# Attention scores in three bf16 parts on 64 rows a head, where it was two fp32 parts on 32 rows

## The chip, the cores and the metric

One core of one Trainium2 chip runs the whole program. The metric is the time of one execution in microseconds of device time, median of the runs. Lower is better.

## The reference

Two transformer layers on x of 4 x 512 x 128 with 16 heads of width 8. Layer 0 has causal attention and a top-1 expert network, layer 1 has self-attention, a "recursive" attention of its output to two stored past states, a gate, and a top-2 expert network. Only the two attentions matter here. Cut to that:

```python
# layer 0, for each of 4 batches and 16 heads, T = 512, dh = 8
q, k, v = split(h @ Wqkv.T)
dots = einsum('bhid,bhjd->bhij', q, k) * dh ** -0.5
attn = softmax(where(causal_mask, -inf, dots))
x = x + ga * (einsum('bhij,bhjd->bhid', attn, v) @ Wout.T + bout)
# layer 1
scores = einsum('bhsd,bhtd->bhst', q, k) * SCALE          # not causal
output = (softmax(scores) @ v) @ Wo + bo
rq = output @ Wrq + brq                                     # from the output of self-attention
rscores = einsum('bhsd,pbhtd->pbhst', rq, past @ Wrk + brk) * SCALE   # two past states of 256
rctx = mean over p of softmax(rscores) @ (past @ Wrv + brv)
```

## The kernel before

The program is one hand-written order of phases (`plan()`), which every engine walks through in turn and issues its own part of; the engines wait for each other by semaphores. `play` steps through generators: a `yield` ends a step, and a generator's start step is a number of STEPS0, STEPS1, FRONT, BACK, KPREP and QPREP (lines 18 to 73). So a phase is due at a step, not at a time.

Attention goes by units: four heads of one batch. Layer 0 has 16 units, layer 1 has 32, of which 16 are recursive (L1_SEQ: self 0, self 1, rec 0, self 2, rec 1, self 3, rec 2, rec 3, four units each). A unit takes 16 steps. It has two halves, which run on different units at the same time:

- `front`: 16 plain scores, phase `mx` (tile t of 128 queries, head j), into a PSUM bank of the ring of four; VectorE reduces each to row maxima (line 2206, recursive line 2199; in layer 0 line 2203, a custom operation that adds the mask, with a read of its accumulator). Then `mcol` splits the maxima in a high and a low part on VectorE, `mT` transposes them on TensorE, ScalarE evicts them to Ms, and `mput` on SP writes them by DMA into rows of the query tile Qs (line 1224).
- `back`: 16 transposed scores, phase `st` (chunk c of 128 keys, head j), which wait for the maxima in Qs, into three PSUM banks; ScalarE takes the exponential to Et (line 1623); in layer 0 GpSimd cuts the diagonal (line 1386); then the value matmuls `pv` and `pva` (line 1898), four heads side by side in columns of 32.

In layer 0 front starts at step 16u + 10 and back at 16u + 35; in layer 1 at 12 and 40.

A head's 8 numbers are made into 32 rows, so that one fp32r matmul sums all the products of high and low parts: rows 0 to 7 high, 8 to 15 low and 16 to 23 high in the queries (for the keys high, high, low), and rows 24 up hold the maxima in the queries and -1 in the keys. The parts are made thus: ScalarE evicts the projection to Xq or Xk, VectorE masks the low 12 bits away (`high`, line 2060, phase `split`), GpSimd subtracts (phase `low`, lines 1327 and 1330, in two halves), SP writes three pieces to Dq or Dk in DRAM (`stage`, lines 1174 to 1183), and reads a unit's four heads back as 128 rows (`ldq`, `ldk`).

In layer 1 keys lie in KT (or RKT for past states) as 4 x 32 rows and head j's matmul uses rows 32j to 32j + 31 alone. In layer 0 they lie block-diagonally in Kbd, three tiles of 128 x 4 x 512 that GpSimd clears at the start; a head's `st` takes all 128 rows of Kbd and Qs, zeros included, and so does its `mx`. Four DMAs a unit fill one Kbd tile.

The first unit of each layer takes no way over DRAM: extra projections `k0`, `q0` (`k1`, `q1`) with weight columns laid out as the 32 rows (u0, u1) go through ScalarE (U0k, U0q) and VectorE (T, lines 2152 to 2175) into Kbd 0 or KT 0 and Qs 0. ScalarE copies three heads and GpSimd one to Kbd (`k0put`). The past keys are split by VectorE (`pastkv`) into kst, doubled by GpSimd (`past2`) and transposed to RKT in four phases `pastK`.

The lines of the score matmuls:

```python
r = slice(32 * j, 32 * j + 32) if l else slice(0, 128)
keys = RKT[r, g, :] if kind == "rec" else KT[u % NK][r, :] if l else Kbd[u % 3][:, j, :]
nc.tensor.matmul(bank(ph)[:, q0:512], keys[:, c * 128:(c + 1) * 128], Qs[q_no(l, u) % NQ][r, q0:512], ...)
```

## Time and profile before

| | us |
|---|---|
| median of 3 runs | 945.59 |
| lowest, highest | 942.89, 954.91 |
| profiled execution | 943.85 |
| its span, first to last instruction | 942.1 |
| attention of layer 0 | 38 to 250 |
| experts of layer 0 | 250 to 332 |
| attention of layer 1, with the start of it | 332 to 795 |
| experts of layer 1 | 795 to 942 |

In the profile PE is TensorE's matmuls, PEld its weight loads, DVE is VectorE, ACT ScalarE, POOL GpSimd and SP the queue of SyncE; a q behind an engine's name is its instruction queue, such as one that issues DMAs. Times are us from the span's start unless marked ns. "idle before" is the time in which the engine stood still just ahead of an instruction, and behind the arrow is what ended that. The ends of matmuls are modelled, so the spacing of starts says more than the durations. PEclk is the share of 2.4 GHz that TensorE's clock was granted; there are two levels, 1 and 0.5. Each unit of either layer takes some 13 us.

### The profile page before, as it was taken

The numbers are of one execution on the slowest core, as the hardware profiler recorded it, in microseconds if no ns is written. First come the engines' busy times: TensorE is split into PE (matmuls) and PEld (weight loads), VectorE is DVE, ScalarE is ACT, GpSimd is POOL, SyncE is SP. The second block draws the span as 40 slices with busy tenths as digits, with TensorE's granted clock in tenths as the row PEclk, the third lists the DMA queues.
The fourth block names the chain that finished last, engine by engine and source line by source line (L and its number), as shares of the span: only waits on it lengthen the run. The fifth ranks groups of instructions, "written<-read, shape, count | busy, mean of one in ns | idle before, by whom it ended". The sixth has DMA issues, their size and how long they took to land.

```text
span 942.1 us, 18341 instructions
## 1 busy us (share of the span) xinstructions
PE 834.8 (89%) x6319; PEld 501.3 (53%) x6319; DVE 720.9 (77%) x2077; ACT 546.7 (58%) x1202; POOL 282.3 (30%) x424
## 2 busy tenths in 40 slices
PE   7698999888879869999999999999987989898994
PEld 6354655455579733344344434344432434788994
DVE  5777788887265768898899888989895874786674
ACT  2355656546556524688788868687664765333431
POOL 6233334326412354204210011001025223344332
PEclk9799999998979966799999979799795988988997
DMA  5556523111103133244242403110251100102123
GB/s 156 189 169 195 179 80 108 41 47 36 43 21 96 56 102 125 72 160 145 112 151 69 136 25 105 47 58 25 83 177 51 47 7 21 42 27 78 42 64 113
DMA packets 68470, 82.43 MB, mean 87 GB/s; under 512 B 8295, under 2 KB 44391, under 8 KB 68057
## 3 DMA queue, kind: packets, MB, share of 16 engines
q1 hardware_dynamic: 40120, 46.11, 16.2%
q10 hardware_dynamic: 24960, 28.32, 9.6%
q0 software_dynamic: 3296, 6.82, 2.2%
...
q14 instruction: 44, 0.35, 0.1%
...
## 4 chain that ended last, share of the span: by engine, by line
PE 55%; DVE 27%; issue 4%; DMA 4%; ACT 4%; POOL 3%; another core or an unknown queue 1%; SPq 1%; ACTq 1%; DVEq 0%; POOLq 0%
PE pv L1898 13%; PE st L1875 10%; DVE M L2199 9%; PE ring L2013 6%; PE ring L1866 5%; PE ring L1769 4%; DVE M L2206 4%; PE st L1998 4%; DVE ring L2203 3%; ACT Et L1623 2%; PE ring L1837 2%; PE st L2006 2%; PE st L1991 2%; PE pv L2006 2%; PE ring L1780 1%
## 5 line engine op out<-in xcount | busy, mean ns | idle before, releaser
L1623 ACT ACTIVATE Et<-st 128x512 f32<-128x512 f32 (+3 forms) x768 | 372.9, 545 | 149.8 <-PE st L1875 130.1
L2206 DVE TENSOR_REDUCE M<-ring 128x1 f32<-128x512 f32 x256 | 159.4, 683 | 29.8 <-PE ring L1866 23.6
L2199 DVE TENSOR_REDUCE M<-ring 128x2 f32<-128x512 f32 x256 | 159.9, 681 | 15.4 <-PE ring L1866 14.7
L1898 PE MATMUL pv<-Et,Va 128*32 128x256 f32 (+3 forms) x1536 | 146.5, 443 | 4.0 <-ACT PVs L1630 2.3
L2203 DVE CUSTOM_DVE_ANT_0 ring<-ring,maskw 128x128 f32<-128x128 f32 (+3 forms) x256 | 120.5, 512 | 36.0 <-PE ring L1866 33.5
L1875 PE MATMUL st<-Qs,Kbd 128*128 128x512 f32 (+3 forms) x256 | 90.0, 370 | 8.9 <-ACT Et L1623 7.5
L1898 PE MATMUL pv<-Et,RV 128*32 128x256 f32 x1024 | 92.4, 434 | 5.1 <-ACT PVs L1630 5.0
L1866 PE MATMUL ring<-Kbd,Qs 128*128 128x128 f32 (+3 forms) x256 | 84.6, 360 | 13.5 <-DVE M L2203 5.9
L1386 POOL TENSOR_SCALAR_AFFINE_SELECT Et<-Et 128x256 f32<-128x256 f32 x128 | 53.0, 419 | 128.0 <-ACT Et L1623 127.7
L1866 PE MATMUL ring<-RKT,Qs 32*128 32x512 f32 x256 | 84.4, 540 | 3.9 <-DVE M L2199 2.3
L1866 PE MATMUL ring<-KT,Qs 32*128 32x512 f32 x256 | 79.0, 553 | 8.9 <-DVE M L2206 8.3
L1875 PE MATMUL st<-Qs,RKT 32*128 32x512 f32 x256 | 78.2, 549 | 5.7 <-ACT Et L1623 5.7
L1875 PE MATMUL st<-Qs,KT 32*128 32x512 f32 x256 | 79.6, 547 | 0.1
L2013 PE MATMUL ring<-w2d,hbuf 128*128 128x128 f32 x552 | 75.4, 282 | 0.7 <-issue 0.7
L1875 PEld LDWEIGHTS st<-Qs,Kbd 128*128 128x128 f32 x256 | 49.2, 195 | 49.9 <-ACT Et L1623 33.1
L2013 PEld LDWEIGHTS ring<-w2d,hbuf 128*128 128x128 f32 x552 | 70.2, 199 | 1.2 <-issue 1.2
L1898 PEld LDWEIGHTS pv<-Et,Va 128*32 128x32 f32 x1536 | 33.8, 112 | 60.9 <-issue 43.5
L1866 PEld LDWEIGHTS ring<-Kbd,Qs 128*128 128x128 f32 x256 | 49.9, 200 | 28.1 <-DVE M L2203 14.3
L1461 POOL DMA_INDIRECT Zd<-Yt,dst x39 | 41.8, 1072 | 65.4 <-ACT Yt L1745 63.7
L1424 POOL DMA_INDIRECT Xd<-fh,pos x48 | 47.6, 991 | 36.2 <-DVE pos L2521 17.4
L1875 PEld LDWEIGHTS st<-Qs,RKT 32*128 32x128 f32 x256 | 32.2, 200 | 46.5 <-issue 25.4
L1327 POOL TENSOR_TENSOR Xq<-Xq,hq 128x256 f32<-128x256 f32 x24 | 18.9, 803 | 123.7 <-DVE hq L2060 121.8
...
## 6 DMA issues: line engine op xcount, KB each, us to landing
...
```

Of the source, the lines that this page charges most:

```text
L1386: e.affine_select(diag, diag, [[0, 2], [1, 128]], ALU.is_ge, 0.0, base=0, channel_multiplier=-1).then_inc(cut_done, 1)
L1424: e.indirect_dma_start(Xd1 if l else Xd0[g], bass.IndirectOffsetOnAxis(r["pos"][:, i, n:n + 1], 0), B.fh[PARTS[q][n // 4]][:, n % 4, :], N ...
L1461: e.indirect_dma_start(Zd, bass.IndirectOffsetOnAxis(B.dst[:, k:k + 1], 0), B.Yt[n % 4][:, :], None).then_inc(y_stored[1][n % 4], 16)
L1623: e.activation(Et[s // 2 % 4][:, j % 2, q0:512], bank(ph)[:, q0:512], ACT.Exp, scale=SCALE).then_inc(exp_done, 1)
L1769: ins = nc.tensor.transpose(bank(ph)[:, t * 128:(t + 1) * 128], src(t), ident[:, :])
L1866: nc.tensor.matmul(bank(ph)[:, 0:n], Qs[q_no(l, u) % NQ][r, t * 128:(t + 1) * 128], keys[:, 0:n], start=True, stop=True).then_inc(mx_full, 1)
L1875: nc.tensor.matmul(bank(ph)[:, q0:512], keys[:, c * 128:(c + 1) * 128], Qs[q_no(l, u) % NQ][r, q0:512], start=True, stop=True).then_inc(st ...
L1898: ins = nc.tensor.matmul(pv[32 * j:32 * j + 32, cols], v, Et[s // 2 % 4][:, j % 2, cols], start=first and (l == 0 or what == "pva"), stop= ...
L2013: ins = nc.tensor.matmul(bank(ph)[:, 0:128], B.hbuf[n % 3][:, f, :], B.w2d[weight_set(l, n)][:, f, :], start=(f == 0), stop=(f == 3))
L2199: e.tensor_reduce(M[i][:, t, j, :], bank(ph)[:, :].rearrange("p (two n) -> p two n", two=2), AX.X, ALU.max).then_inc(mx_red, 1)
L2203: e.tensor_tensor_reduce(bank(ph)[:, 0:n], bank(ph)[:, 0:n], maskw[:, 512 - n:512], 1.0, -3e38, ALU.add, ALU.max, M[i][:, t, j, 0:1]).then ...
L2206: e.tensor_reduce(M[i][:, t, j, 0:1], bank(ph)[:, 0:n], AX.X, ALU.max).then_inc(mx_red, 1)
```

## The change

A number is now the sum of three bf16 parts. A head has 64 rows: for each of its 8 numbers eight rows, six of them for the products of parts that are kept (QPARTS, KPARTS), one (MAXROW) for the maxima, which have three parts too, one empty. Two heads lie in the 128 rows of a tile and two more behind them in the free dimension (Qs, KT and RKT are 128 x 2 x 512 in bf16, as many bytes as before). Layer 0 uses the same KT tiles as layer 1; Kbd with its clearing, its four loads a unit and `k0put` is gone. The order of `mx` and `st` and the steps of front and back stay as they are.

VectorE's `split` makes the first part by a copy to bf16, GpSimd's `low` subtracts, a new phase `mid` on VectorE copies the second part, a new phase `last` on GpSimd subtracts for the third. For the first batch of each layer VectorE does all eight operations within `split`. Each part is written once for all its places by a DMA that repeats it (3, 2 and 1 times). The first unit of each layer is made from the parts on chip by `sel`: three matmuls with a 0/1 matrix (`pick`) for each half of queries and keys; ScalarE evicts the keys and adds the -1 row (kcol), VectorE the queries. `mT` is now a matmul on the upper halves of the fp32 words, and `mput` has three DMAs, six for recursive units, where it had two and four.

```diff
+QPARTS, KPARTS = (0, 0, 0, 1, 1, 2), (1, 0, 2, 0, 1, 0)
+HR, MAXROW = 64, 6
...
-        for piece in range(6 if keys else 3):
-            if piece < (4 if keys else 2):
-                do("low", l, b, k, piece)
-            do("stage", l, b, k, piece)
+        if k == 0:
+            for piece in (0, 3, 1, 4, 2, 5):
+                do("stage", l, b, k, piece)
+                yield
+            return
+        for side in range(1 + keys):
+            do("low", l, b, k, 2 * side)
+            do("low", l, b, k, 2 * side + 1)
+            do("stage", l, b, k, 3 * side)
             yield
+        if keys:
+            yield
+        do("mid", l, b, k)
+        yield
+        for side in range(1 + keys):
+            do("last", l, b, k, 2 * side)
+            do("last", l, b, k, 2 * side + 1)
+            do("stage", l, b, k, 3 * side + 1)
+            yield
+        for side in range(1 + keys):
+            do("stage", l, b, k, 3 * side + 2)
...
-    do("clear", "Kbd0")
-    do("clear", "Kbd1")
     do("hT", 0, 0)
     do("warm", 2)
     do("brow", 1)
-    do("k0")
-    do("q0")
-    for what in ("pq", "pk"):
+    for what in ("pq", "pk", "split"):
         do(what, 0, 0, 0)
-    do("k0put")
+    for s in range(2):
+        do("sel", 0, "k", s)
+        do("sel", 0, "q", s)
...
-            do("pastK", g)
-            yield from wait((6, 14, 4, 4)[g])
+            for s in range(2):
+                do("pastK", g, s)
+                yield from wait((3, 7, 2, 2)[g])
...
+        def rows_of(j):
+
+            return slice(HR * (j % 2), HR * (j % 2) + HR)
...
-                    if piece in (0, 1):
+                    of = (Dq[k % 2] if piece < 3 else Dk[n % 2]).rearrange("h (r a) n -> (h r) a n", a=8)
+                    if piece == 0:
                         sp.wait_ge(q_high, n + 1)
-                        e.dma_start(Dq[k % 2][:, 16 * piece:16 * piece + 8, :], hq[:, :]).then_inc(q_staged, 16)
+                        e.dma_start(of[:, 0:3, :], Pq[0][:, :].unsqueeze(1).broadcast_to([128, 3, 512])).then_inc(q_staged, 16)
+                    elif piece == 1:
+                        sp.wait_ge(q_mid, n + 1)
+                        e.dma_start(of[:, 3:5, :], Pq[1][:, :].unsqueeze(1).broadcast_to([128, 2, 512])).then_inc(q_staged, 16)
                     elif piece == 2:
-                        sp.wait_ge(q_low, 2 * n + 2)
-                        e.dma_start(Dq[k % 2][:, 8:16, :], Xq[:, :]).then_inc(q_staged, 16)
-                    elif piece in (3, 4):
+                        sp.wait_ge(q_last, 2 * n + 2)
+                        e.dma_start(of[:, 5, :], Pq[2][:, :]).then_inc(q_staged, 16)
...
-                    wide = 4 if units[l][u][0] == "rec" else 2
+                    many = 2 if units[l][u][0] == "rec" else 1
                     q = Qs[q_no(l, u) % NQ]
                     sp.wait_ge(*taken(("mT", l, u)))
-                    for m in range(wide):
-                        e.dma_start(q[24 + m:128:32, :].bitcast(F32), Ms[l][u % 2][16 * m:16 * m + 16, :]).then_inc(m_in[u % 2], 16)
+                    for m in range(NPART * many):
+                        m16 = 32 // many * m
+                        e.dma_start(q[8 * m + MAXROW:128:HR, :, :], Ms[l][u % 2][m16:m16 + 16, :]).then_inc(m_in[u % 2], 16)
...
+                elif what == "last":
+                    l, b, k, piece = a
+                    n0 = 256 * (piece % 2)
+                    sl = slice(n0, n0 + 256)
+                    if piece < 2:
+                        pool.wait_ge(q_mid, n_split["split", l, b, k] + 1)
+                        e.tensor_tensor(Pq[2][:, sl], Xq[:, sl], Pq[1][:, sl], ALU.subtract).then_inc(q_last, 1)
+                    else:
+                        pool.wait_ge(k_mid, n_ksplit["split", l, b, k] + 1)
+                        e.tensor_tensor(Pk[2][:, sl], Xk[:, sl], Pk[1][:, sl], ALU.subtract).then_inc(k_last, 1)
...
+                elif what == "sel":
+                    l, of, s = a
+                    pe.wait_ge(ld["pick"], 16)
+                    if of == "k":
+                        pe.wait_ge(k_last, 2 * n_ksplit["split", l, 0, 0] + 2)
+                    else:
+                        pe.wait_ge(q_last, 2 * n_split["split", l, 0, 0] + 2)
+                    parts, n0 = (Pq, 0) if of == "q" else (Pk, 6)
+                    for i in range(NPART):
+                        ins = nc.tensor.matmul(bank(ph)[:, :], pick[:, n0 + 3 * s + i, :], parts[i][0:32, :], start=(i == 0),
+                                               stop=(i == NPART - 1))
+                    ins.then_inc(misc_full, 1)
...
-                    nc.tensor.transpose(bank(ph)[:, 0:128], Mc[l][u % 2][:, :], ident[:, :]).then_inc(misc_full, 1)
+                    parts = M[:, u % 2:u % 2 + NPART, :].rearrange("p i n -> p (i n)")
+                    nc.tensor.matmul(bank(ph)[0:96, 0:128], tops(parts), tops(ident[:, :]), start=True, stop=True).then_inc(misc_full, 1)
...
-                    keys = RKT[r, g, :] if kind == "rec" else KT[u % NK][r, :] if l else Kbd[u % 3][:, j, :]
+                    r, s = rows_of(j), j // 2
+                    keys = RKT[r, g, s, :] if kind == "rec" else KT[u % NK][r, s, :]
                     pe.wait_ge(*m_ready(l, u))
-                    nc.tensor.matmul(bank(ph)[:, q0:512], keys[:, c * 128:(c + 1) * 128], Qs[q_no(l, u) % NQ][r, q0:512],
+                    nc.tensor.matmul(bank(ph)[:, q0:512], keys[:, c * 128:(c + 1) * 128], Qs[q_no(l, u) % NQ][r, s, q0:512],
...
-                    high(hq[:, :], Xq[:, :]).then_inc(q_high, 1)
-                    if has_keys(l, k):
-                        n = n_ksplit[ph]
+                    e.tensor_copy(Pq[0][:, :], Xq[:, :]).then_inc(q_high, 1)
+                    if nk is not None:
                         dve.wait_ge(*taken(("pk", l, b, k)))
-                        if n:
-                            dve.wait_ge(k_staged, 48 * n)
-                        high(hk[:, :], Xk[:, :]).then_inc(k_high, 1)
+                        if nk:
+                            dve.wait_ge(k_staged, 48 * nk)
+                        e.tensor_copy(Pk[0][:, :], Xk[:, :]).then_inc(k_high, 1)
+                    if k == 0:
+                        dve.wait_ge(q_high, n + 1)
+                        e.tensor_tensor(Xq[:, :], Xq[:, :], Pq[0][:, :], ALU.subtract).then_inc(q_low, 2)
+                        dve.wait_ge(k_high, nk + 1)
+                        e.tensor_tensor(Xk[:, :], Xk[:, :], Pk[0][:, :], ALU.subtract).then_inc(k_low, 2)
+                        dve.wait_ge(q_low, 2 * n + 2)
+                        e.tensor_copy(Pq[1][:, :], Xq[:, :]).then_inc(q_mid, 1)
+                        dve.wait_ge(k_low, 2 * nk + 2)
+                        e.tensor_copy(Pk[1][:, :], Xk[:, :]).then_inc(k_mid, 1)
+                        dve.wait_ge(k_mid, nk + 1)
+                        e.tensor_tensor(Pk[2][:, :], Xk[:, :], Pk[1][:, :], ALU.subtract).then_inc(k_last, 2)
+                        dve.wait_ge(q_mid, n + 1)
+                        e.tensor_tensor(Pq[2][:, :], Xq[:, :], Pq[1][:, :], ALU.subtract).then_inc(q_last, 2)
...
+                elif what == "mid":
+                    l, b, k = a
+                    sp_ = ("split", l, b, k)
+                    dve.wait_ge(q_low, 2 * n_split[sp_] + 2)
+                    e.tensor_copy(Pq[1][:, :], Xq[:, :]).then_inc(q_mid, 1)
+                    if sp_ in n_ksplit:
+                        dve.wait_ge(k_low, 2 * n_ksplit[sp_] + 2)
+                        e.tensor_copy(Pk[1][:, :], Xk[:, :]).then_inc(k_mid, 1)
...
-                    halves(hi, lo, M[u % 2][:, :, :, :] if kind == "rec" else M[u % 2][:, :, :, 0]).then_inc(mcol_done, 1)
+                    step(e.tensor_tensor(m1, m0, tops(m0), ALU.subtract))
+                    settle()
+                    e.tensor_tensor(m2, m1, tops(m1), ALU.subtract).then_inc(mcol_done, 1)
...
-                    halves(k4[:, t, :, 8:16], k4[:, t, :, 16:24], bank(ph)[:, 0:128].rearrange("p (h r) -> p h r", r=8))
+                    settle()
+                    step(e.tensor_copy(k4[:, :, 1], keys))
+                    settle()
+                    step(e.tensor_tensor(pastR[:, :], keys, k4[:, :, 1], ALU.subtract))
+                    settle()
+                    step(e.tensor_copy(k4[:, :, 0], pastR[:, :]))
+                    settle()
+                    step(e.tensor_tensor(k4[:, :, 2], pastR[:, :], k4[:, :, 0], ALU.subtract))
```

## Rows read from the trace of the kernel before

**Rows 1.** The page: the span, busy time by engine, and TensorE's clock in 40 slices

```profile
span 942.1 us, 18341 instructions
...
PE 834.8 (89%) x6319; PEld 501.3 (53%) x6319; DVE 720.9 (77%) x2077; ACT 546.7 (58%) x1202; POOL 282.3 (30%) x424
...
PEclk9799999998979966799999979799795988988997
```

**Rows 2.** Busy time by stage: stretch, length, us (instructions) by engine, PEclk, DMA share, GB/s

```profile
38.00:250.00 212.00, 187.81 (x1202) 112.72 (x1201) 160.08 (x672) 122.27 (x332) 84.18 (x168) 0.96 0.34 100
...
360.00:795.00 435.00, 409.26 (x3414) 175.35 (x3414) 370.77 (x813) 314.80 (x608) 84.72 (x118) 0.88 0.26 85
```

**Rows 3.** Chain that ended last, by line: first 38 to 250, then 360 to 795

```profile
by line: PE st L1875 12.1%; PE pv L1898 11.9%; DVE ring L2203 11.8%; PE ring L1866 6.7%; DMA Qs<-Ms 5.0%; issue 4.8%; ACT Et L1623 4.5%; PE ring L1769 3.1%; PE ring L1837 2.8%; POOL Xd L1424 2.8%; POOL Et L1386 2.2%; DMA Kbd<-Dk 2.0%; DVE f
...
by line: PE pv L1898 21.7%; DVE M L2199 20.6%; PE st L1875 15.0%; DVE M L2206 7.4%; PE ring L1866 5.9%; PE ring L1769 4.5%; issue 2.6%; ACT Et L1623 2.3%; PE ring L1780 1.8%; another core or an unknown queue 1.6%; PE st L1853 1.5%; PE ring 
```

**Rows 4.** Timeline of TensorE, layer 1, full clock: start us, us, instruction, tiles, forms

```profile
530.46 0.64 PE L1898 MATMUL pv<-Et,Va 128*32 128x256 f32 x8
531.03 0.50 PE L1875 MATMUL st<-Qs,KT 32*128 32x512 f32 x2
531.04 0.50 PE L1866 MATMUL ring<-KT,Qs 32*128 32x512 f32 x2
531.47 0.45 PE L1898 MATMUL pv<-Et,Va 128*32 128x256 f32 x4
```

**Rows 5.** The same timeline in layer 1 at the low clock

```profile
602.67 0.79 PE L1866 MATMUL ring<-KT,Qs 32*128 32x512 f32 x2
...
603.40 1.08 PE L1898 MATMUL pv<-Et,RV 128*32 128x256 f32 x8
604.41 0.79 PE L1875 MATMUL st<-Qs,RKT 32*128 32x512 f32 x2
```

**Rows 6.** Timeline of TensorE in layer 0

```profile
157.43 0.39 PE L1875 MATMUL st<-Qs,Kbd 128*128 128x512 f32 x1
157.66 0.40 PE L1866 MATMUL ring<-Kbd,Qs 128*128 128x512 f32 x1
157.89 0.34 PE L1875 MATMUL st<-Qs,Kbd 128*128 128x384 f32 x1
...
160.27 0.22 PE L1866 MATMUL ring<-Kbd,Qs 128*128 128x128 f32 x1
...
160.50 0.22 PE L1866 MATMUL ring<-Kbd,Qs 128*128 128x128 f32 x1
```

**Rows 7.** VectorE: a run of maxima (timeline); masked maximum (groups: busy us, mean ns)

```profile
484.17 7.25 DVE L2199 TENSOR_REDUCE M<-ring 128x2 f32<-128x512 f32 x12
...
L2203 DVE CUSTOM_DVE_ANT_0 ring<-ring,maskw 128x512 f32<-128x512 f32 x64 | 43.4, 716 | 7.8 <-PE ring L1866 7.2 <-issue 0.5
```

**Rows 8.** Instructions of one line (ns min/median/max); then a weight load in groups

```profile
L2060 DVE TENSOR_SCALAR hq<-Xq x12: 417/419/426, 18.3 to 688.7; 128x512 int32<-128x512 int32 x12
...
L1327 POOL TENSOR_TENSOR Xq<-Xq,hq x24: 721/733/1249, 19.4 to 689.9; 128x256 f32<-128x256 f32 x24
...
L1875 PEld LDWEIGHTS st<-Qs,KT 32*128 32x128 f32 x256 | 33.4, 199 | 41.5 <-issue 28.7 <-ACT Et L1623 10.3
```

**Rows 9.** Timeline of the opening

```profile
17.47 0.75 DVE L2155 SCALAR_TENSOR_TENSOR Qs<-T,u,U0q 128x512 fp32r<-128x512 f32 x1
...
19.50 3.09 PE L1866 MATMUL ring<-Kbd,Qs 128*128 128x128 f32 x11 [0.68 <-ACT Kbd L1567]
...
29.88 0.60 ACT L1480 ACTIVATE modB<-ring 128x512 f32<-128x512 f32 x1 [9.90 <-issue]
```

**Rows 10.** Timeline around the maxima of unit 7 of layer 0

```profile
127.69 1.09 SPq L1224 DMA_DIRECT2D Qs<-Ms  x2
...
131.30 0.39 PE L1875 MATMUL st<-Qs,Kbd 128*128 128x512 f32 x1
```

**Rows 11.** Timeline where layer 1 starts

```profile
339.67 1.29 DVE L2206 TENSOR_REDUCE M<-ring 128x1 f32<-128x512 f32 x2 [5.62 <-POOL rstd L1372]
```

333 lines of the change are left out of this document (136 added, 197 removed).

## The prediction

> **What bounds the kernel now.** I read five views, from the whole to one step. The page first: TensorE counts as busy for 89% of the span, VectorE for 77%, and the granted clock is below full speed in a good part of the slices [rows 1]. Then the busy time by stage [rows 2]: attention of layer 0 (38 to 250) takes 212 us, attention of layer 1 (360 to 795) takes 435 us, and together they are two thirds of the kernel; the change touches little outside of them. The chain of work that ended last, cut to these stretches, says who sets the pace [rows 3]: in layer 0 the score matmuls (st and the ring's L1866) hold 18.8% of 212 us, 40 us; in layer 1 they hold 20.9%, the value matmuls 21.7% and VectorE's maxima 28%. So no single engine bounds it. TensorE's order is fixed, it waits in order for banks that VectorE and ScalarE free, and whichever has most to do in the next few steps sets the pace.
>
> The single step shows why. In layer 1 a step is two transposed scores, two plain scores, eight value matmuls. At full clock the value matmuls start at 530.46, the next scores at 531.03, the next value matmuls at 531.47 [rows 4]: 0.57 for values, 0.44 for all four scores, which start within 0.01 us of each other because each has its own 32 rows of the array. That is 1.01 us a step. VectorE needs more: twelve maxima in a row took 7.25 us [rows 7], 1.21 us for the two of a step. At the low clock (1.2 GHz, half speed) the same step took 0.73 for the scores (602.67 to 603.40) and 1.01 for the values, 1.74 us [rows 5], and there TensorE is the bound. The clock's mean in the stage is 0.88 [rows 2], so 24% of it ran at the low level. In layer 0 there is no such overlap: each score takes the whole array, a 512-column one 0.23 us (157.43 to 157.66 to 157.89), and a step of two 128- and 256-column ones 0.23 us (160.27 to 160.50) [rows 6].
>
> **The change, part by part.** The sum is made against the profiled execution, 943.85 us (span 942.1); the median of the runs shown is 945.6, 1.7 above, and I add the sum to the median.
>
> *Layer 0 scores.* A head now takes 64 rows, so two fit side by side. The hand-written order has st and mx of one step at heads of opposite parity (front starts at step 10, back at 35, and 25 is odd), so they lie in different halves and can run together. A step then costs the longer of the two. A large step (512 and 512 or 384) goes from about 0.43 to 0.23, a small one from 0.23 to perhaps 0.15: 0.32 to 0.19 on average, 2.1 us over 16 steps, 34 us of TensorE time over 16 units. What of this is on the path? At most that share of the chain's 40 us: 2.1 of 5.1, 16 us, to which some waits behind it may add, 22 as the bound. Nothing as the other bound: a 512-column masked maximum takes VectorE 0.72 us [rows 7], more than TensorE's step before, and VectorE is busy 160 of 212 us [rows 2]. I take a third of 34: **-12**.
>
> *Layer 1 scores.* Here the change takes parallelism away: four heads of 32 rows become two pairs of 64 rows, and the second pair streams after the first. The trace has no bf16 matmul; the nearest row for streaming 512 columns through more than 32 rows is layer 0's 0.23 [rows 6], of which 0.21 are columns (512 at 2.4 GHz). So of the 0.44 of a step's scores 0.21 is streaming and 0.23 is loading the weights and changing between scores and values. The second pair adds 0.21, or less by what bf16 weights load faster: bounds 0.21 (nothing) and 0.01 (the whole 0.199 of a load [rows 8]). The operand is half as wide, so I take a third of the load, and +0.14. At the low clock, likewise, 0.43 more streaming less 0.08: +0.35. There are 8 x 32 = 256 steps, 61 of them at the low clock by the stage's mean: 195 x 0.14 = 27 and 61 x 0.35 = 21, 48 us of TensorE time. At full clock a step becomes 1.15, still under VectorE's 1.21, so most is covered by the maxima; that cover is gone wherever a projection or a transpose has put TensorE behind, and I leave a quarter exposed, +7. At the low clock all is exposed, +21. Against that TensorE has more to do per step, and if that keeps the clock up, low steps disappear, each with its 0.35 and with the 0.53 that it now costs over VectorE's pace (61 x 0.53 = 32). I take a third of them gone: 7 + 14 - 11 = **+10**; bounds -25 (all gone, 7 - 32) and +48 (none gone, nothing covered).
>
> The Trainium skill speaks for the cheaper end: "TensorE: Matmul & The Clock Gate", section "Weight-path perf modes", says that a weight of 128 columns that is not fp32 is read some two times faster, as measured. By it half of the load would go, the step would grow by 0.11 and the term would be some 2 us smaller. The trace before has only 4-byte weights and can't show it.
>
> *Opening.* The first keys and queries came from two extra projections and four VectorE operations. Qs was written at 17.47 and the first score ran at 19.50 [rows 9]. Now VectorE makes all parts before anything is selected: four copies and four subtractions, 4 x 0.42 + 4 x 0.72 = 4.6 us (a copy as the 0.42 of [rows 8], a subtraction as the nearest pass over two operands of 512, 0.72 [rows 7]), where T and Qs took some 3 us. 12 selecting matmuls of 0.21 follow, 2.6 us, half of them behind the last subtraction, and an eviction of Qs. 1.6 + 1.3 + 0.3 makes the first score some 3 us later, near 22.6. ScalarE's later queue of loads, which held modB until 29.88 and TensorE with it [rows 9], starts behind its evictions and moves too. **+3**.
>
> *Start of layer 1.* The same split and selection replace k1 and q1, between the last expert tiles: VectorE some 2 us more, TensorE 1 us more. VectorE's first maxima wait for rstd until 339.67 [rows 11], behind the gathers, so much is hidden: +1.5. The past keys take four small VectorE steps a tile for two, and eight transposes and evictions for four: +1.5. Together **+3**.
>
> *Staging.* Ten q splits and six k splits get one more VectorE copy, 16 x 0.42 = 6.7 us, and GpSimd twice its subtractions, 0.73 each [rows 8]. Six of 16 lie in layer 0, where GpSimd also cuts the diagonal ahead of the value matmuls. **+5** (0 to 10). Bytes to Dq, Dk stay the same; four Kbd loads a unit become one.
>
> *Maxima.* Three parts for two: one more DMA a unit (two more for recursive ones) on SP, 0.55 each (two took 1.09) [rows 10]. What is late next is the unit's first st: in that unit it ran 2.5 us after the second issue. Where the slack is near that size, some five units of layer 0, it is +0.55; layer 1 mostly has 4 us or more. SP has nothing queued behind that is due sooner. **+3** (0 to 9, all units of layer 0, if layer 0 gets faster and uses the slack up).
>
> Sum: -12 + 10 + 3 + 3 + 5 + 3 = +12. 945.6 + 12 = **958 us**.
>
> **Rivals.**
> (A) Layer 1 becomes bound by TensorE. For: the stage's TensorE counts 409 of 435 us as busy, and with projections and transposes its real load is close to VectorE's 371 [rows 2]; a longer step then shows in full. Against: at full clock 1.15 is still under 1.21. It decides where the pair's step passes 1.21, with 0.20 more a step. Price: 48 for 10 in layer 1, 945.6 + 50 = 996 at the worst, 977 half way from the forecast.
> (B) Faster. Layer 0 gives its bound of 22 and layer 1 keeps the full clock, because TensorE has more to do there: -22 in layer 0, 7 - 32 in layer 1, +14 for the rest is -33: 913; with half of the low steps gone, 7 + 11 - 16 in layer 1, 939. For: at 1.74 us a low step is the dearest thing in the stage. Against: the low stretch at 602 had TensorE busy throughout and did not rise for it.
> (C) The clock falls in layer 0, where it now is 0.96 [rows 2]: TensorE has 2.1 us less to do in each unit. A quarter of the stage at the low level, with steps some 40% longer as in layer 1 (1.74 for 1.21), is +21: 979. The Trainium skill has the rule behind it ("TensorE: Matmul & The Clock Gate", "What's actually happening": the slow clock is the default and activity releases it).
> (D) The change does not do what it says: halves don't run together. Then layer 1's scores take two more passes, 0.43 a step, and a step is 1.6: 256 x 0.4 = 100 us more, 1050.
>
> **How the numbers follow.** The forecast (945 to 970) has 0.40, A 0.25, B 0.20, C 0.10, D 0.05. 2% of the median, about what a measurement can tell, is 19: under 927 counts as faster, over 964 as slower. Faster: three quarters of B, 0.15. Slower: A, C and D without their mild ends, and the top of the forecast, 0.37. Same: 0.48. The range 925 to 985 leaves out D, the worse third of A and the better third of B, 0.2.
>
> **What would show it.** In layer 0, st and mx of a step starting within 0.02 us of each other and steps of 0.23; the stage at about 200 us for 212. In layer 1, first pair and second pair 0.2 us apart, 0.55 to 0.60 from the first score to the value matmuls, twelve maxima in a row still at 7.25 us where the clock is full; the stage at about 450. First score near 22.6. The clock's means by stage, 0.96 and 0.88 before, decide between A, B and C. I am wrong if layer 1's steps stay at 1.0 to 1.2 and the stage gets shorter, or if the load of bf16 weights leaves nothing exposed in either layer.

## The result and the profile after

The changed kernel takes 970.5 us (median of four runs, 965.3 to 972.8), the kernel before 945.4 (median of four too, 942.9 to 954.9): a ratio of 1.0234, interval 1.0176 to 1.0292: slower, and whether by more or less than 2% stays open. The profiled execution of the changed kernel took 972.8 us.

The page of the changed kernel, for [rows 1]:

```profile
span 971.1 us, 18448 instructions
...
PE 827.0 (85%) x6351; PEld 414.3 (43%) x6351; DVE 736.8 (76%) x2107; ACT 545.8 (56%) x1203; POOL 293.4 (30%) x450
...
PEclk8679999887579976879999999999987898978997
```

The busy time of the two attention stages, for [rows 2] (columns as there):

```profile
41.00:250.00 209.00, 171.49 (x1146) 62.27 (x1146) 166.23 (x698) 115.52 (x315) 84.39 (x167) 0.86 0.35 104
364.00:817.00 453.00, 404.40 (x3424) 135.15 (x3424) 394.39 (x839) 315.94 (x610) 112.64 (x158) 0.92 0.26 84
```

Weight loads went from 501 us to 414, TensorE's matmuls hardly changed, and the clock moved in opposite directions: 0.96 to 0.86 in layer 0, 0.88 to 0.92 in layer 1.

To see where the 29.0 us between the two spans lie, I took the start of the first exponential of a unit from ScalarE's timeline (all 768 are recorded) and made differences. "Opening" ends at the first one, "layer 0" goes from unit 0 to unit 15, "experts" from there to the first of layer 1, "start" over its first four units, "rest" from its unit 4 to its unit 31. The labels below are experiments of the next section.

| kernel | opening | layer 0 | of it units 5 to 10 | experts | start | rest | tail |
|---|---|---|---|---|---|---|---|
| before | 38.4 | 199.4 | 58.8 | 124.0 | 53.4 | 365.9 | 161.0 |
| changed | 49.8 | 200.9 | 58.9 | 136.4 | 57.8 | 366.4 | 159.8 |
| changed, second chip (e5) | 49.2 | 203.1 | 58.4 | 134.8 | 57.8 | 350.4 | 149.4 |
| e1 order of the opening | 42.7 | 198.0 | 58.0 | 135.4 | 57.8 | 351.5 | 153.6 |
| e2 order of layer 1's start | 49.0 | 205.2 | 58.4 | 123.4 | 58.0 | 350.6 | 150.1 |
| e3 layer 0 whole array | 47.2 | 194.5 | 58.2 | 127.9 | 57.8 | 350.2 | 151.4 |
| e4 layer 1 four side by side | 49.6 | 201.0 | 58.5 | 130.2 | 55.9 | 351.5 | 152.8 |
| e6 layer 0 with fill | 49.9 | 212.4 | 64.3 | 131.0 | 57.9 | 350.8 | 150.0 |
| e7 no mid, no last | 47.5 | 198.6 | 59.1 | 133.2 | 57.5 | 351.0 | 149.0 |
| e8 two maxima | 47.5 | 200.5 | 58.1 | 134.7 | 57.8 | 349.0 | 150.3 |
| e9 block-diagonal, bf16 | 45.2 | 195.8 | 58.5 | 131.2 | 59.2 | 362.4 | 159.7 |
| e10 past keys on GpSimd | 49.1 | 199.5 | 58.4 | 136.2 | 55.0 | 363.5 | 159.1 |
| e11 combined | 42.3 | 194.3 | 58.5 | 119.4 | 54.8 | 363.7 | 158.3 |
| e12 combined, mid on ScalarE | 42.1 | 192.1 | 58.0 | 123.6 | 53.3 | 363.1 | 159.5 |

Changed less before: +11.4, +1.5, +12.4, +4.4, +0.5, -1.2. The loss is in three places: the opening, the way from layer 0's attention to layer 1's, and the first units of layer 1, where the past keys are made; these columns hold less than a quarter of the time. The two long stretches of scores, on which most of the prediction went, gave almost neither gain nor loss in sum. In layer 1 that sum is made of opposites, as the starts of its units and the clock's record show: from its unit 4 to its unit 14, where neither trace leaves the full clock, the changed kernel takes 122.0 us for 119.3; from 14 to 24, where the kernel before is at the low level for 28 us and the changed one for 3, 130.9 for 135.0; over the last seven, with 31 us at the low level for 44, 113.4 for 111.6.

Two cautions. The two profiled executions took 972.8 and 943.85 us where the medians are 970.5 and 945.4, so some 4 of the 29 us are spread between executions. And each line of the table is one execution: traces that share the code of a stretch have 47.2 to 49.9 us in the opening (nine of them), 198.0 to 205.2 in layer 0 (six) and 130.2 to 136.4 in the experts (five), so a difference in a column means something only beyond that. "Rest" and "tail" must be compared on one kind of chip only: e1 to e8 ran on chips where the kernel before takes 923 to 925 us, e9 to e12 where it takes 947 to 948, as in the first comparison.

**Opening.** TensorE's timeline of the changed kernel, then the two instructions that began it, on VectorE and GpSimd, for [rows 9]:

```profile
14.80 3.69 PE L1851 MATMUL ring<-hT,wqkv 128*128 128x512 f32 x4
22.39 1.43 PE L1843 MATMUL ring<-Pk,pick 32*128 32x512 bf16 x3 [3.91 <-DVE Pk L2185]
...
26.19 1.48 PE L1843 MATMUL ring<-Pq,pick 32*128 32x512 bf16 x3
27.60 2.07 PE L1861 MATMUL ring<-wqkv,hT 128*128 128x128 f32 x8
29.46 1.91 PE L1822 MATMUL pv<-onesM 128*128 128x128 f32 x8
31.31 0.40 PE L1881 MATMUL ring<-KT,Qs 64*128 64x128 bf16 x4
```
```profile
9.89 2.60 DVE L2144 TENSOR_SCALAR xh<-x,mv,rstd 128x128 f32<-128x128 f32 x4 [3.02 <-POOL rstd L1393]
9.82 2.01 POOL L1306 MEMSET Va<- 128x2304 f32 x1
```

The first score comes at 31.31, not at 22.6. TensorE stands still 3.91 us while VectorE makes the parts, and then runs the twelve selections at the low level, 1.27 us for three of them (22.39 to 26.19 for three groups). In e8 the same wait was followed by six selections at full clock, 0.65 us for three, and six at the low level, which is part of the spread of the opening. The value projection and the warm-up stand behind the selections, so 3.7 us more. xh took 2.60 us where it took 1.11 before: since the clearing of Kbd is gone, which had waited for xh, GpSimd clears Va in the same 2 us.

**Start of layer 1.** TensorE, then VectorE, for [rows 11]:

```profile
344.13 1.43 PE L1843 MATMUL ring<-Pk,pick 32*128 32x512 bf16 x3 [3.94 <-DVE Pk L2185]
345.36 1.48 PE L1843 MATMUL ring<-Pq,pick 32*128 32x512 bf16 x3
346.77 2.08 PE L2028 MATMUL ring<-w2d,hbuf 128*128 128x128 f32 x8
...
357.82 2.84 PE L2028 MATMUL ring<-w2d,hbuf 128*128 128x128 f32 x24
```
```profile
365.95 3.68 DVE L2217 TENSOR_REDUCE M<-ring 128x1 f32<-128x512 f32 x6 [3.66 <-POOL rstd L1393]
```

The same 3.94 us of standing still, and behind it selections and expert tiles at the low level (a group of eight takes 2.08 us, at full clock 1.06). The last outputs of the experts, the gathers behind them, rstd and the first maxima all come later, 365.95 for 339.67.

**Past keys.** VectorE in the kernel before, one tile, and in the changed one:

```profile
387.02 0.29 DVE L2060 TENSOR_SCALAR kst<-ring 128x128 int32<-128x128 int32 x1
387.34 0.29 DVE L2065 TENSOR_TENSOR kst<-ring,kst 128x128 f32<-128x128 f32 x1
387.55 0.28 DVE L2688 COPY RV<-ring 128x128 f32<-128x128 f32 x1
```
```profile
412.74 0.72 DVE L2699 CAST kst<-ring 128x128 bf16<-128x128 f32 x1
413.49 0.38 DVE L2701 TENSOR_TENSOR pastR<-ring,kst 128x128 f32<-128x128 f32 x1
413.91 0.45 DVE L2703 CAST kst<-pastR 128x128 bf16<-128x128 f32 x1
414.39 0.72 DVE L2705 TENSOR_TENSOR kst<-pastR,kst 128x128 bf16<-128x128 f32 x1
415.15 0.29 DVE L2707 COPY RV<-ring 128x128 f32<-128x128 f32 x1
```

2.70 us a tile for 0.81. Writing bf16 into every eighth place costs up to 0.72 for 128 columns; an operation over 512 columns that lie side by side takes 0.42 [rows 8].

**The scores.** Layer 0 at full clock, and a step of layer 1 at full clock, for [rows 6] and [rows 4]:

```profile
168.16 0.39 PE L1881 MATMUL ring<-KT,Qs 64*128 64x512 bf16 x1
...
168.67 0.39 PE L1881 MATMUL ring<-KT,Qs 64*128 64x512 bf16 x1
168.68 0.33 PE L1890 MATMUL st<-Qs,KT 64*128 64x384 bf16 x1
```
```profile
527.15 0.39 PE L1890 MATMUL st<-Qs,RKT 64*128 64x512 bf16 x2
527.37 0.38 PE L1881 MATMUL ring<-KT,Qs 64*128 64x512 bf16 x2
527.68 0.64 PE L1913 MATMUL pv<-Et,RV 128*32 128x256 f32 x8
528.25 0.39 PE L1890 MATMUL st<-Qs,RKT 64*128 64x512 bf16 x2
```

In layer 0 the two heads start 0.01 us apart, as forecast. But the steps do not follow each other in 0.23 us: those around these rows start at 167.20, 167.64, 168.16 and 168.67, 0.44 to 0.52 apart, where the kernel before needed 0.46 (157.43 to 157.89). In layer 1 the second pair follows 0.22 behind the first, the values at 0.53, and a step is 1.10 us for 1.01. A weight load, from the page's groups, for the last of [rows 8]:

```profile
L1890 PEld LDWEIGHTS st<-Qs,KT 64*128 64x128 bf16 x512 | 34.5, 95 | 114.9 <-ACT Et L1635 54.7
```

### The profile page after: what moved, and what is told of

The parts are those of the page before. It is cut to its first block, busy times and chain, and to the rows that moved or that the text cites. A ratio compares the mean times of both kernels' runs of the same rounds, so it can differ in the third digit from the quotient of the medians.

```text
span 971.1 us, 18448 instructions
## 1 busy us (share of the span) xinstructions
PE 827.0 (85%) x6351; PEld 414.3 (43%) x6351; DVE 736.8 (76%) x2107; ACT 545.8 (56%) x1203; POOL 293.4 (30%) x450
## 4 chain that ended last, share of the span: by engine, by line
PE 52%; DVE 29%; issue 5%; ACT 4%; DMA 4%; POOL 3%; another core or an unknown queue 1%; SPq 1%; ACTq 1%; DVEq 0%; POOLq 0%
PE pv L1913 11%; DVE M L2210 9%; PE st L1890 6%; PE ring L2028 5%; DVE M L2217 5%; PE ring L1881 5%; PE ring L1781 4%; PE st L2013 4%; DVE ring L2214 2%; ACT Et L1635 2%; DMA Qs<-Ms 2%; PE ring L1851 2%; PE st L2021 2%; PE pv L2021 2%; PE st L2006 2%
## 5 line engine op out<-in xcount | busy, mean ns | idle before, releaser
L1881 PE MATMUL ring<-KT,Qs 64*128 64x512 bf16 (+3 forms) x512 | 132.3, 375 | 21.2 <-DVE M L2214 8.7
L1890 PE MATMUL st<-Qs,KT 64*128 64x512 bf16 (+3 forms) x512 | 125.5, 371 | 16.8 <-ACT Et L1635 12.8
L1890 PEld LDWEIGHTS st<-Qs,KT 64*128 64x128 bf16 x512 | 34.5, 95 | 114.9 <-ACT Et L1635 54.7
L1881 PE MATMUL ring<-RKT,Qs 64*128 64x512 bf16 x256 | 63.6, 393 | 7.2 <-DVE M L2210 5.4
L1890 PE MATMUL st<-Qs,RKT 64*128 64x512 bf16 x256 | 58.8, 403 | 10.5 <-ACT Et L1635 9.3
L1881 PEld LDWEIGHTS ring<-KT,Qs 64*128 64x128 bf16 x512 | 35.6, 96 | 69.3 <-DVE M L2214 24.6
L1448 POOL DMA_INDIRECT Xd<-fh,pos x48 | 47.5, 990 | 36.4 <-DVE pos L2532 17.8
L1338 POOL TENSOR_TENSOR Xq<-Xq,Pq 128x256 f32<-128x256 f32 x20 | 13.7, 706 | 102.0 <-DVE Pq L2169 102.0
L2013 PE MATMUL st<-XsT,w1d 128*128 128x128 f32 x312 | 43.6, 283 | 1.0 <-issue 0.8
L1757 ACT ACTIVATE Yt<-ring,wt 128x128 f32<-128x128 f32 x39 | 14.3, 367 | 52.6 <-PE ring L2028 43.3
L1913 PEld LDWEIGHTS pv<-Et,RV 128*32 128x32 f32 x1024 | 21.2, 111 | 53.1 <-issue 42.0
```

The lines of the kernel that those rows point to most:

```text
L1448: e.indirect_dma_start(Xd1 if l else Xd0[g], bass.IndirectOffsetOnAxis(r["pos"][:, i, n:n + 1], 0), B.fh[PARTS[q][n // 4]][:, n % 4, :], N ...
L1881: nc.tensor.matmul(bank(ph)[:, 0:n], Qs[q_no(l, u) % NQ][r, s, t * 128:(t + 1) * 128], keys[:, 0:n], start=True, stop=True).then_inc(mx_fu ...
L1913: ins = nc.tensor.matmul(pv[32 * j:32 * j + 32, cols], v, Et[s // 2 % 4][:, j % 2, cols], start=first and (l == 0 or what == "pva"), stop= ...
L2013: ins = nc.tensor.matmul(hb[2 * i][:, fs], B.w1d[ws][:, fs], xt, start=True, stop=True)
```

## The experiments

Each kernel is an edit of the changed kernel. Kernels e1 to e4 ran on one chip, e5 to e8 on another of the same level, e9 to e11 on a third and e12 on a fourth; ratios are to the kernel before on the same chip.

**e1.** Opening: what has its inputs already goes ahead of the selections, and GpSimd waits for xh before it clears.

```diff
-    for what in ("pq", "pk", "split"):
+    for what in ("pq", "pk", "split", "vp"):
         do(what, 0, 0, 0)
+    do("warm", 3)      # 8 matmuls, was 4
     for s in range(2):
         do("sel", 0, "k", s)
         do("sel", 0, "q", s)
-    do("vp", 0, 0, 0)
     do("loads")
-    do("warm", 3)
...
                 elif what == "clear":
+                    pool.wait_ge(xh_done, 1)
                     clear_va(1)
```

> Edit to the changed kernel, opening only: the value projection and eight warm-up matmuls (four more than before) go ahead of the selecting matmuls instead of behind them, and GpSimd's clearing of the second Va tile waits for xh, so that it doesn't run beside VectorE's four xh operations. Theory 'starts' (the 9.6 us by which layer 0 starts later are the chain Xk, split, select, value projection, warm-up, first score, partly at the low clock): xh back from 2.60 to about 1.1 us, first score near 26 where it was 31.3, first transposed score about 4 us earlier, and the end moves with it: about 966 where the changed kernel has 970.5, ratio to the kernel before near 1.019. Rival 'hidden' (the unit behind is held by something else, modB or the maxima's way): first score earlier, but the first transposed score stays near 47.6 and the time stays at 970 (1.023).

Measured 1.0183 (1.0143 to 1.0224), 5 us under the control e5. TensorE's timeline:

```profile
16.94 1.95 PE L1822 MATMUL pv<-onesM 128*128 128x128 f32 x16
20.12 0.80 PE L1843 MATMUL ring<-Pk,pick 32*128 32x512 bf16 x3 [1.23 <-DVE Pk L2185]
...
23.84 0.40 PE L1881 MATMUL ring<-KT,Qs 64*128 64x128 bf16 x4 [0.83 <-DVE Qs L2159]
```

(The profile shows each of these fp32 matmuls as two, so x16 are the eight of the warm-up.) The selections take 0.65 us for three instead of 1.28, xh is back at 1.11, and the first score runs at 23.84, earlier than the 26 that was expected. The first exponential gains 6.5 us and the end follows (span 939.0 for 944.7). The theory of the starts holds: what is lost there is not made up later. How much of the gain is the order and how much the wait for xh (1.5 us of it by itself) was not taken apart.

**e2.** Start of layer 1: vp and more expert tiles go ahead of the selections.

```diff
-        for what in ("pq", "pk", "split"):
+        for what in ("pq", "pk", "split", "vp"):
             do(what, 1, 0, 0)
             yield
-        for s in range(2):
-            do("sel", 1, "k", s)
-            do("sel", 1, "q", s)
-            yield
-        do("vp", 1, 0, 0)
-        yield
-        yield from stage(1, 0, 0)
+        for n, _ in enumerate(stage(1, 0, 0)):
+            if n in (2, 3):
+                do("sel", 1, "k", n - 2)
+                do("sel", 1, "q", n - 2)
+            yield
```

> Edit to the changed kernel, start of layer 1 only: the selecting matmuls stand two and three steps later in the order, behind the value projection and further expert tiles, so that TensorE has work while VectorE makes the parts. Theory 'starts' (of the 12.8 us between the end of layer 0's attention and the first maxima of layer 1 most is TensorE standing 3.9 us before the first selection, then expert tiles and selections at the low clock): that gap closes, the clock stays up, last expert output some 7 us earlier (near 353), ratio 1.015, about 963. Rival 'gathers' (the maxima wait for rstd behind the last Yd stores and gathers, which do not depend on this order): last expert output earlier by less than 2 us and the time unchanged, 1.023.

Measured 1.0108 (1.0064 to 1.0153), 12 us under the control's ratio. TensorE:

```profile
342.85 1.06 PE L2026 MATMUL ring<-w2d,hbuf 128*128 128x128 f32 x8
344.03 0.80 PE L1841 MATMUL ring<-Pk,pick 32*128 32x512 bf16 x3
...
347.90 2.94 PE L2026 MATMUL ring<-w2d,hbuf 128*128 128x128 f32 x24
350.77 0.95 PE L1879 MATMUL ring<-KT,Qs 64*128 64x512 bf16 x4
```

VectorE's parts are ready at the same time as before (344.03 for 344.13), but TensorE has worked until then and all that follows runs at full clock: the last outputs at 347.90 instead of 357.82. "Experts" goes from 134.8 to 123.4, the value of the kernel before. So the 12.4 us were neither the added operations (4.0 us of VectorE, which are still there) nor the gathers, but an order that made TensorE wait, and the low clock after the wait.

**e3 and e6.** What side by side is worth in layer 0. e3 gives each score all 128 rows, so heads can't run together; e6 keeps them side by side and adds matmuls of ones.

```diff
-                    r, s = rows_of(j), j // 2
+                    r, s = rows_of(j) if l else slice(0, 128), j // 2     # e3, in mx and in st
...
 def ones_ahead(ph):
-    return 0
+    return int(ph[0] == "mx" and ph[1] == 0 and ph[4] % 2 == 0)           # e6
```

> Edit to the changed kernel, layer 0 only: each score matmul takes all 128 rows instead of its head's 64, so that two heads' scores are added together (the output is not the reference's) and st and mx can't run side by side. As many instructions and bytes as before. The prediction's term (running side by side takes 12 us off the stage, with the clock as it was): the stage from 209 to about 221, ratio 1.036, about 982. Theory 'clock' (what side by side saves is given back, because TensorE is granted full speed less often: 0.86 of the stage instead of 0.96): the granted clock's mean goes back up to about 0.95, and the stage stays at 209 within 3 us, 1.023. Theory 'other engines' (VectorE and the waits between engines set the pace, TensorE's time doesn't matter): stage unchanged, whatever the clock does.

> Edit to the changed kernel, layer 0 only: one 128x128 fp32 matmul of ones, whose result is overwritten, ahead of every second plain score (128 of them, 0.27 us each at full clock by the warm-up matmuls, 34 us of TensorE time, as much as running side by side took away). The scores keep running side by side. Theory 'clock' (the kernel gained 11 us when two heads took the whole array, because TensorE with more to do is granted full speed): the clock's mean in the stage goes from 0.86 to about 0.95 and the ratio to about 1.012, as with the whole array. Rival 'order' (side by side itself does harm, by making exponentials and maxima come in bunches): the clock rises but the time doesn't fall, 1.023 or, with 34 us of extra work partly exposed, up to 1.035.

e3: 1.0118 (1.0071 to 1.0164). e6: 1.0493 (1.0418 to 1.0567). The control, e5:

> The changed kernel without any edit, as the control on this chip for the runs beside it: the chips differ in level (the kernel before took 945 us on the first and 925 on the chip of the first four experiments), so what an edit is worth is read against this one. All theories: ratio to the kernel before 1.023, within its interval of 1.018 to 1.029.

Measured 1.0238 (1.0167 to 1.0309). The exponentials that fit into a stretch tell the pace of layer 0. Columns: stretch, length, then TensorE, weight loads, ScalarE (the exponentials) and GpSimd, of these instructions alone, clock, DMA. The kernel before, then e5, then e3, each at 110 to 180 and 180 to 238:

```profile
110.00:180.00 70.00, 19.38 (x192) 4.50 (x192) 36.26 (x97) 19.56 (x49) 1.00 0.36 108
180.00:238.00 58.00, 13.99 (x128) 3.02 (x128) 25.04 (x65) 13.44 (x33) 0.91 0.13 39
```
```profile
110.00:180.00 70.00, 24.45 (x192) 5.74 (x192) 36.50 (x96) 19.86 (x47) 1.00 0.39 120
180.00:238.00 58.00, 17.70 (x120) 3.23 (x120) 22.41 (x61) 12.28 (x30) 0.68 0.11 34
```
```profile
110.00:180.00 70.00, 23.66 (x200) 5.30 (x192) 36.43 (x97) 20.44 (x48) 1.00 0.37 109
180.00:238.00 58.00, 14.16 (x132) 3.31 (x128) 24.83 (x64) 13.04 (x32) 0.91 0.14 43
```

At full clock all three make 96 or 97 exponentials in 70 us, and units 5 to 10 take 58.2 to 58.8: running two heads side by side buys nothing there. The second stretch shows the clock, 0.68 side by side and 0.91 with the whole array. Its exponentials, 61 for 64, settle nothing, since the stretch catches each kernel at another place (the changed kernel's first trace has 64 there at 0.74, e9 62 at 0.95). The stage does: 203.1 us for 194.5, with 60 us at the low level for 17. Of these 8.6 us 5.5 lie between the starts of units 0 and 3 (46.7 us for 41.2, 16 us at the low level for none) and 3.4 between those of units 10 and 13 (48.5 for 45.1, 30 us for 7). It is no accident of one trace: the six traces with the changed kernel's layer 0 have 48 to 60 us at the low level and take 198.0 to 205.2, the four in which a score takes the whole array (e3, e9, e11, e12) have 14 to 17 and take 192.1 to 195.8. So the prediction's -12 was not merely too large: it has the other sign, which none of e3's three expectations had either. The experts behind it, where the edit touches nothing, also got 6.9 us shorter, with TensorE at the low level from 249 to 273 in e5 and for 3 of these us in e3; but that column spreads by 6 us among kernels without such an edit, so only the low level, and not the 6.9, can be put down to e3.

e6 shows the other half. With the fill the clock is full (0.99 in 180 to 238), so it is TensorE's load that decides it. But the time rises, against both of its forecasts, by 9 us in layer 0 of the profiled execution. That execution, at 953.7, was the fastest; the median is 966.7, and what the other 13 us are no trace shows. For the 9 us TensorE's timeline gives the reason:

```profile
142.31 0.49 PE L1801 MATMUL ring<-onesM 128*128 128x128 f32 x2
142.73 0.23 PE L1881 MATMUL ring<-KT,Qs 64*128 64x128 bf16 x2
```

One fill (x2, as the profile shows a fp32 matmul as two) takes 0.42 us in its place, not the 0.27 that I had worked with, 128 of them 54 us, and each stands ahead of a score for which VectorE waits. Load is only worth adding where TensorE waits. By the Trainium skill ("TensorE: Matmul & The Clock Gate", "What's actually happening") throttling is the default and activity releases it; e3 and e6 agree, with 0.91 and 0.99 for 0.68. The Trainium skill's "TensorEngine Tiling (Array Packing)", "When to Use Tiling", names row tiling for contractions of up to 64; here that gave no time at full clock.

**e4.** Layer 1 with 32 rows a head, four at a time, half of the products left out.

```diff
-                    r, s = rows_of(j), j // 2
+                    r, s = (slice(32 * j, 32 * j + 32), 0) if l else (rows_of(j), j // 2)
```

> Edit to the changed kernel, layer 1 only: each head's score matmul takes 32 of its rows instead of 64, so four heads run side by side as in the kernel before (half of the products are left out, and the exponential's scale is made 1024 times smaller so that nothing overflows; the output is not the reference's). The prediction's term (two pairs in turn cost 10 us in layer 1): the stage from 453 to about 443, ratio 1.013, about 960. Theory 'VectorE's pace' (twelve maxima in 7.25 us are 1.21 a step, the longer TensorE step of 1.11 hides under it): steps of 1.01 on TensorE, but the stage stays at 453 within 3 us, 1.023. Theory 'clock' (the longer steps keep the clock up, 0.92 for 0.88): the mean clock falls to 0.88 and the stage gets longer, by up to 10 us.

Measured 1.0235 (1.0188 to 1.0283), the control's ratio. The step is shorter on TensorE (values 0.38 us behind the first score, where the pairs need 0.53), the clock over 410 us of the stage is 0.90 instead of 0.97, and "rest" is 351.5 for 350.4. Two effects cancel in it. From unit 4 to 14 of layer 1, still mostly at full clock, e4 is 1.2 us shorter than e5 (120.3 for 121.5); over the last seven units, with 27 us at the low level for 10, it is 1.9 longer (100.2 for 98.3). So the pairs cost next to nothing in sum, and what the shorter step gives is paid back in clock. That VectorE's maxima set the pace at full clock fits that, with 1.21 us a step in [rows 7], more than TensorE's 1.01 and 1.10; no run changed VectorE's part to show it.

**e7 and e8.** Staging and maxima: e7 leaves the third part of queries and keys out from the second batch on, e8 writes two parts of the maxima.

```diff
-  e.tensor_tensor(Xq[:, sl], Xq[:, sl], Pq[0][:, sl], ALU.subtract).then_inc(q_low, 1)
+  e.tensor_tensor(Pq[1][:, sl], Xq[:, sl], Pq[0][:, sl], ALU.subtract).then_inc(q_low, 1)   # e7; keys alike, mid and last empty
...
                     for m in range(NPART * many):
+                        if m // many == (2, 1)[u % 2]:
+                            continue                                                          # e8
```

> Edit to the changed kernel: from the second batch of each layer on the third part of queries and keys is left out (GpSimd writes the difference as the second part, the copies of mid and the subtractions of last are gone, the third piece that is staged is that of the first batch; the output is a little off the reference). The prediction's term: staging costs 5 us (0 to 10), so 1.018, about 5 less than the unchanged kernel. Rival 'hidden' (the copies stand where VectorE waits for scores anyway and GpSimd has room): less than 2 us, 1.022 or more. Rival 'clock' (less work elsewhere changes nothing for TensorE): the clock's means stay at 0.86 and 0.96 in the two attention stages.

> Edit to the changed kernel: only two of the three parts of the maxima are written to the queries, so mput has two DMAs a unit and four a recursive one, as in the kernel before (the third part is missing, which moves the scores by less than their rounding). The prediction's term: 3 us (0 to 9), so 1.020. Rival 'hidden' (only units whose first transposed score waits for these rows can show it, 3.1 us of such waits in all of layer 0): less than 1 us, 1.023.

e7: 1.0149 (1.0084 to 1.0215), 8 us; its layer 0 is 4.5 us shorter and nothing moves in layer 1. All four executions of e7 (935.6 to 938.6) lie below all four of e5 on the same chip (942.5 to 948.5), so something is gained; but 1.7 us of it are in the opening, which the edit doesn't touch, and 198.6 in layer 0 is inside the spread of kernels without it. e8: 1.0209 (1.0138 to 1.0280), 3 us, with the same 1.7 in the opening, and its executions overlap with e5's. So both sizes agree with the prediction's (5 and 3), that of e7 roughly, and e8's can't be told from nothing.

**e9.** One part of the change undone: keys of layer 0 block-diagonal, but in bf16.

```diff
+        Kb = [at(f"Kb{i}", [128, 4, 512], BF16, kbd0 + 4096 * i) for i in range(3)]
...
+                        for h in range(2):
+                            e.dma_start(Kb[u % 3][64 * h:64 * h + 64, h::2, :],
+                                        Dk[slot][4 * g:4 * g + 4, :, :].rearrange("(s two) r n -> two r s n", two=2)[h]
+                                        ).then_inc(kb_in[u % 3], 16)
...
-                        keys = KT[u % NK][r, s, :]
+                        keys = KT[u % NK][r, s, :] if l else Kb[u % 3][:, j, :]
```

> One part of the change undone, with the reference's output: in layer 0 the three-part bf16 keys lie block-diagonally again (three tiles of 128 x 4 x 512 in bf16, cleared by GpSimd, two loads a unit, the first unit's keys evicted in two halves) and a score matmul takes all 128 rows, zeros included; layer 1 stays as changed. Theory 'clock' (side by side leaves TensorE so little to do that it is granted full speed less often, and buys nothing where the clock is full, since there VectorE and the waits set the pace: units 5 to 10 took 58.4 us side by side and 58.2 with the whole array): the clock's mean in layer 0's attention 0.95 where side by side has 0.86, the stage some 8 us shorter, ratio near 1.012. Rival 'not the array' (the gain of the whole-array run came from its wrong scores or from its chance phases of the clock, or the second load and the clearing take it back): 1.020 or more.

Measured 1.0138 (1.0065 to 1.0211), 9 us under the control's ratio. Against the changed kernel on a chip of the same level: layer 0 195.8 for 200.9, with 17 us at the low level for 54, and experts 131.2 for 136.4; against e10 on the same chip layer 0 195.8 for 199.5. The opening is 45.2 for 49.8, and that is not the block's: here too the clearing waits for xh, which takes 1.11 us again, and the first six selections ran at full clock. So with the reference's scores, the second load and the clearing in it the whole array keeps the clock up, and 4 to 5 us of e3's 9 in the stage stand. The 5 in the experts are inside that column's spread.

**e10.** Past keys: VectorE copies, GpSimd makes the parts.

```diff
-                    step(e.tensor_copy(k4[:, :, 1], keys))     # and three more, on VectorE
+                    e.tensor_copy(pastR[:, t, :], keys)        # the four now in past2 on GpSimd, a tile at a time
```

> Edit to the changed kernel, past keys only: VectorE copies the projected keys of a tile and GpSimd makes the three parts, where VectorE made them in four operations of 0.38 to 0.73 us (2.7 us a tile with the values' copy, 0.8 in the kernel before). Theory 'VectorE in the way' (TensorE waits for VectorE's copy behind them in the ring of banks, so they stand on the path; unit 18 to unit 19 of the count over both layers takes 18.4 us where the kernel before took 11.6): that unit back to about 13, all later ones 5 us earlier, ratio 1.018. Rival 'clock' (the stretch is slow because it runs at the low clock, 13.7 of its 18 us): less than 2 us, 1.022 or more.

Measured 1.0189 (1.0114 to 1.0263), 5 us, by an interval that overlaps with the control's. The table shows 2.8 in "start", and that column is steady: 55.0, 54.8 and 53.3 in the three kernels with this edit (e10, e11, e12), 57.5 to 59.2 in the others but e4. Unit 18 to 19 did not get shorter (17.6 us), the one before did, 12.5 for 15.9. The edit took VectorE's 1.9 us a tile away and put a new wait there, in TensorE's timeline:

```profile
423.56 0.58 PE L2052 MATMUL ring<-ident,kst 128*128 128x128 bf16 x4 [3.52 <-POOL kst L1432]
424.08 1.08 PE L1917 MATMUL pv<-Et,Va 128*32 128x256 f32 x8
```

GpSimd needs 4.1 us a tile and is done at 423.4; the transposes were due at 420. TensorE stands 3.52 us, and the clock falls again (1.08 for eight value matmuls). Starting the transposes some steps later should give the rest; it was not tried.

**e11 and e12.** e1, e2, e9 and e10 together, and then the mid copies on ScalarE.

```diff
-                    dve.wait_ge(q_low, 2 * n_split[sp_] + 2)
-                    e.tensor_copy(Pq[1][:, :], Xq[:, :]).then_inc(q_mid, 1)
+                    act.wait_ge(q_low, 2 * n_split[sp_] + 2)
+                    e.activation(Pq[1][:, :], Xq[:, :], ACT.Copy).then_inc(q_mid, 1)      # e12; keys alike
```

> All four edits that gave or should give time, with the reference's output: order of the opening (5 us), order of the start of layer 1 (12), keys of layer 0 block-diagonal in bf16 (11), past keys on GpSimd (5). If they add up: 1.0238 - 0.0055 - 0.013 - 0.012 - 0.005 = 0.988, about 1% faster than the kernel before. If they share a cause (the clock at the start of layer 1 was also better in the whole-array run, so the second and the third may count the same microseconds twice): 0.995 to 1.000. If the rest of the change (staging, maxima, steps of layer 1) is a net loss: not under 1.000.

> The combined kernel with one more edit: the copies of the second part (mid) are made by ScalarE instead of VectorE, 16 copies of 128x512 (10 of queries, 6 of keys). Leaving out the second copy and the third subtraction had given some 8 us (1.0149 for 1.0238). Theory 'VectorE's copies' (what staging costs are 16 x 0.42 = 6.7 us on the engine that sets the pace): 5 us less than the combined kernel, ratio near 0.988. Rival 'chain to the queries' (what staging costs is the longer way of the parts through GpSimd and the queues, which stays): ratio 0.993 as before. Rival 'ScalarE in the way' (exponentials wait behind a copy that waits for GpSimd's subtraction, so TensorE's banks come free later): slower than the combined kernel, 0.997 or more.

e11: 0.9932 (0.9899 to 0.9965), faster than both kernels. Added up, the four edits give 1.0238 - 0.0055 - 0.0130 - 0.0100 - 0.0049 = 0.9904, within the interval, and short of the 0.988 that was expected; the xh wait is counted twice in it. Its attention stages:

```profile
42.00:237.00 195.00, 162.28 (x1122) 71.34 (x1135) 159.50 (x666) 114.02 (x314) 84.03 (x168) 0.96 0.36 105
356.00:783.00 427.00, 384.81 (x3409) 130.23 (x3410) 369.64 (x803) 315.89 (x611) 109.41 (x159) 0.95 0.27 85
```

With the clock at 0.96 and 0.95 layer 0 takes 194.3 us for 199.4 before, and the experts' part 119.4 for 124.0. Whether the kernel before would gain from the orders of e1 and e2 too was not tried. e12: 0.9922 (0.9894 to 0.9951), no difference to e11 that could be told, where 0.988 would have been 5 us. So what staging costs is not mainly VectorE's copies. That it is the longer way through GpSimd and the queues fits, but is not shown: only e7 speaks for it, and e7 removes GpSimd's subtractions and the copies at once.

## Where the prediction was right and where wrong

The forecast was 958 with 925 to 985, the result 970.5. The range held, and the likeliest case (945 to 970) was missed by half a microsecond, but that is width and not insight: of the sum only the two small terms at its end are about right. The two terms on scores were to give -2 and came out near +2 with the staging in it, and the two starts with the past keys were to cost 6 and cost 28.

- **Layer 0 scores, -12: wrong in sign.** That st and mx start together came true to 0.01 us, but steps of 0.23 did not: they came 0.44 to 0.52 apart. The step that failed is "what of this is on the path? ... I take a third of 34". I divided TensorE's saving by its share of the chain, but the chain passes through TensorE at those places only because the order has it wait there for others; at full clock five units take 58.9 us for 58.8. Its lower bound, nothing, was right at full clock, and rival C (the clock falls in layer 0) is what happened: 0.86 for 0.96. Its price, 21 us, was too high: e3 and e9 put it at 4 to 9 in the stage, and what it adds in the experts behind (5 to 7 in the table) is not clear of the spread. It should have had more than 0.10: the row against it, VectorE's 0.72 for TensorE's 0.43 a step, was in hand.
- **Layer 1 scores, +10: too high.** The size of the step was right (+0.09 at full clock for a forecast of +0.14; 0.22 between pairs). By the Trainium skill ("TensorE: Matmul & The Clock Gate", "Weight-path perf modes") weights of 128 columns that are not fp32 are read about twice as fast; the trace agrees, with 95 ns for 199. The step that failed is the size of its three pieces, +7, +14 and -11. Exposed at full clock are at most 2.7 us in the ten units where both traces are at full clock, staging and maxima included, and e4 got 1.2 back over the same units. The last seven units, where most of the low steps are left, are 1.8 longer and not 14. And where low steps went, between the starts of units 14 and 24, the time followed: 4.1 us less for 24 us less at the low level, which is rival B's mechanism at a fraction of its price. Together "rest" is +0.5. Rival A falls: the stage hardly feels the step.
- **Opening, +3: mis-sized, +11.4.** The 4.6 us of VectorE were right (17.44 to 22.85, with a wait for Xk in it). I costed the selections at 0.21 each and they ran at 0.42, at the low level, behind 3.91 us in which TensorE stood still; I left out the value projection and the warm-up that the fixed order puts behind them; and I took the clearing of Kbd for a thing that merely goes away, where its wait had kept GpSimd off while VectorE made xh.
- **Start of layer 1, +1.5: mis-sized, +12.4.** "VectorE's first maxima wait for rstd ... so much is hidden" turned out backwards: rstd hangs on gathers, the gathers on the last expert tiles, and those now stood behind the selections in TensorE's order. e2 gives all of it back.
- **Past keys, +1.5: mis-sized, +4.4.** I counted operations and took their duration from a dense one. Of the 4.4 us e10 gets 2.8 back and puts a new wait in their place; that the rest is VectorE's too is not shown.
- **Staging +5, maxima +3: not contradicted** (some 6 to 8 and 3 by e7 and e8, the second not clear of the noise). The reason given for staging, 16 x 0.42 us of VectorE's copies, is at least not the main one: in e12 ScalarE makes them and the time stays.

I had split the change into many small prices and sized them by engine time. What decided was where the order makes TensorE stand still, and at which clock it goes on.
